# Four 32-column tiles for P·V and a second TensorE round for the sums, with PSUM laid out anew

## The chip, the core and the metric

The kernel runs on one core of a Trainium2 chip. The time is the device time of one execution in microseconds (us), as the median of three runs. TensorE (PE) multiplies matrices, VectorE (DVE) reduces and works elementwise, ScalarE (ACT) computes the exponentials, GpSimd (POOL) splits numbers into two parts, SyncE (SP) issues most DMAs.

## The reference

A decoder block in float32 on 4 batches of 1024 tokens, width 512, 16 heads of width 32. Three layers follow one another; each ends with a residual sum and a layer norm. The change touches the first two, which are attentions of one shape:

```python
# layer 0: gated self-attention
attn_align = softmax(einsum('bhqd,bhkd->bhqk', inner, outer) / sqrt(32))
attn = attn_align * aperture[b,h,q,None] * expression[b,h,None,k]   # both sigmoids of x @ W
attn = attn / (attn.sum(axis=-1, keepdims=True) + 1e-8)
converged = einsum('bhqk,bhkd->bhqd', attn, v)                      # then turned and multiplied by Wout
# layer 1: cross-attention on ctx, keys masked
scores = where(mask == 0, -inf-like, q @ k.T / sqrt(32)); p = softmax(scores); out = (p @ v) @ Wo
# layer 2: experts, gates and one causal attention; untouched
```

## The kernel before

`attention(nc, masked, io)` is written once and built twice: layer 0 (`masked` false) and layer 1. Each has a loop over the 4 batches, and in it every engine walks the same list, `attention_steps(masked)`, and does its part of each step. So the order of the list is the order on every engine, and semaphores join the engines.

In a batch come the projections (`Q`, `K`, `V`, and in layer 0 `EX`, `AP` for the gates), each 512-wide product held in one PSUM bank; then 8 pairs of heads; then the output projection `out`, and the transposes `xt` for the next layer.

A pair `p` has 8 steps over the keys, `kt`, of 128 keys each. In one such step stand:
- `st`, two heads: the transposed scores, 128 keys by 1024 queries, 2 matmuls of 512 columns a head (L557); in layer 1 each is followed by a matmul that adds the mask (L562). ACT takes the exponential of 1024 columns at once into `probs` (L781). A ring of two 1024-wide tiles, `scores`, holds them.
- `smax`: the scores the other way round for the next pair, to find each query's maximum. 2 heads by 8 blocks by 2 halves make 32 single matmuls a pair (L627), each into one bank of the 512-wide ring `work`, and DVE reduces each (L977; in layer 1 L973 with the mask). In pair 0 they run at 1 or 2 a gap, since they must be ready ahead; in pairs 6 and 7 they run out.
- `pv`: `v_ext` (32 columns of V, and 2 that give sums) times `probs`, for one half `c` of the queries and both heads, in two tiles of 64 columns (L580). Between the halves stands an `smax`.

After a pair, DVE copies the accumulators to `u` (L859). `den` turns them by 4 transposes a half, so that the sums lie along the partitions (L637); DVE makes 1/sum (L1007 to L1025); `bc` turns that back, spread over 32 rows (L644); DVE multiplies (L1033) into `q_raw`. The last pair's `den` and `bc` run with nothing beside them, and POOL's split (L403, L405) and the `out` step wait for them. In layer 1 DVE adds a correction for absent rows (L995) in pair 7.

`mneg` (L631) turns the maxima into one row, which ACT copies and a DMA puts into the stack for the next pair's `st`.

The matmuls of the projections, `st` and `smax` have float32r operands; `pv`, `den`, `bc` and `mneg` have float32, and the profile records a 512-wide float32 product as two matmuls (2048 in the code, 4096 in the profile).

Of the kernel before, what the change touches and what calls it, by code (L numbers as in the profile page):

```python
# [15 lines left out]
VW = DH + 2  # L16
# [18 lines left out]
def attention_steps(masked):  # L35

    smax = lambda p: [("smax", p, h, t, c) for h in range(2) for t in range(TT) for c in range(NC_)]  # L40
# [18 lines left out]

    GAPS = 4  # L60
    ahead = [m for p in range(1, PAIRS) for m in smax(p)]
    left = 0
    due = []
    for p in range(PAIRS):
        extra = {}
        if p > 0:
# [1728 lines left out]
```

## Time and profile before

| what | value |
|---|---|
| median of 3 runs (lowest, highest) | 5076.81 us (5066.39, 5081.88) |
| profiled execution, first to last instruction | 5068.7 us |
| PE busy | 4480.0 us, 88% |
| DVE busy | 2950.8 us, 58% |
| ACT busy | 1400.0 us, 28% |
| POOL busy | 734.8 us, 14% |
| mean granted TensorE clock | 0.944 of full |

Layers 0 and 1 take the span up to about 4000 us, layer 2 the rest. A matmul's recorded duration holds its latency, and matmuls overlap, so the distance from one start to the next says what one costs, and the busy share overstates how full PE is. An engine's idle time counts only where PE, the engine that is nearly always busy, waits for it.

### The profile page before, as it was taken

What the parts mean: (1) busy time and instruction counts of PE and PEld (TensorE: products, weight loads), DVE (VectorE), ACT (ScalarE), POOL (GpSimd) and SP (SyncE); (2) the same over time, 40 slices, a digit from 0 to 9 for tenths busy, and PEclk for the clock granted to TensorE, in tenths of its full rate; (3) what the DMA queues carried; (4) which work ended last, traced back from release to release, by engine and by line L of the source; (5) the groups of instructions that cost most, each with busy time, mean ns of one, the idle gap of its engine ahead of it and who ended that gap; (6) DMA issues with size and microseconds to landing.
All of it is one profiled execution on the core that took longest, in us unless ns stands there. A gap on an engine that the chain in (4) does not pass through costs nothing. (4 is left out here: it accounts for less than half of the span.)

```text
span 5068.7 us, 60158 instructions
## 1 busy us (share of the span) xinstructions
PE 4480.0 (88%) x19080; PEld 2464.3 (49%) x19080; DVE 2950.8 (58%) x5751; ACT 1400.0 (28%) x1693; POOL 734.8 (14%) x488
## 2 busy tenths in 40 slices
PE   6898899789988977999799979997999598989897
PEld 4334533543363335333543354335433276767676
DVE  3674476367546743664466546653665475757575
ACT  1333234223413421333133312341233302020202
POOL 2102210320021013102210131003100100000000
PEclk9999999899999988999899989998999798999998
DMA  2212211221122214210421042114211300000000
GB/s 81 59 39 73 65 38 51 69 57 38 38 80 59 55 45 139 51 38 26 162 59 37 27 154 57 37 38 144 65 38 30 125 11 33 18 33 19 34 17 17
DMA packets 114496, 285.92 MB, mean 56 GB/s; under 512 B 16240, under 2 KB 18160, under 8 KB 114160
## 3 DMA queue, kind: packets, MB, share of 16 engines
q1 hardware_dynamic: 87648, 213.54, 16.1%
q10 hardware_dynamic: 26512, 68.16, 3.9%
q8 instruction: 178, 2.92, 0.2%
q14 instruction: 158, 1.29, 0.1%
HBM read 137.48 MB, written 42.99 MB: 36 GB/s over the span
## 5 line engine op out<-in xcount | busy, mean ns | idle before, releaser
L781 ACT ACTIVATE probs<-scores 128x1024 f32<-128x1024 f32 x1024 | 1027.3, 1023 | 1637.0 <-PE scores L562 880.0
L580 PE MATMUL acc<-probs,v_ext 128*34 128x512 f32 x4096 | 1064.0, 606 | 1.0 <-DVE u L859 1.0
L627 PE MATMUL work<-stack 96*128 96x512 f32 x1792 | 876.8, 497 | 91.4 <-DVE q_raw L1033 31.2
L973 DVE CUSTOM_DVE_ANT_0 work<-work,mask_q 128x512 f32<-128x512 f32 x896 | 619.8, 704 | 327.9 <-PE work L627 305.2
L557 PE MATMUL scores<-stack 97*128 97x512 f32 x2048 | 785.3, 458 | 4.0 <-ACT probs L781 2.6
L977 DVE TENSOR_REDUCE mx<-work 128x1 f32<-128x512 f32 x896 | 602.8, 689 | 267.1 <-PE work L627 256.0
L627 PEld LDWEIGHTS work<-stack 96*128 96x128 f32 x1792 | 336.9, 190 | 820.3 <-issue 381.2
L518 PE MATMUL work<-stack,w 128*128 128x512 f32 x1536 | 382.7, 411 | 172.8 <-DVEq L871 152.1
L1336 PE MATMUL work_e<-w_in_e,x_e 128*128 128x512 f32 x2304 | 523.4, 389 | 0.0
L1336 PEld LDWEIGHTS work_e<-w_in_e,x_e 128*128 128x128 f32 x2304 | 432.2, 188 | 89.8
L557 PEld LDWEIGHTS scores<-stack 97*128 97x128 f32 x2048 | 396.0, 195 | 102.1 <-ACT probs L781 51.2
L518 PEld LDWEIGHTS work<-stack,w 128*128 128x128 f32 x1536 | 302.6, 199 | 251.0 <-DVEq L871 155.2
L562 PE MATMUL scores<-mask_k,eye 128*128 128x512 fp8e5 x1024 | 406.9, 397 | 0.0
L403 POOL TENSOR_SCALAR qk<-q_raw 128x512 fp32r<-128x512 f32 (+1 forms) x96 | 73.5, 766 | 2120.2 <-DVEq L1038 980.8
L580 PEld LDWEIGHTS acc<-probs,v_ext 128*34 128x34 f32 x4096 | 159.8, 110 | 321.7 <-issue 278.5
L518 PE MATMUL work<-w,qk 128*128 128x512 f32 x768 | 207.8, 423 | 42.8 <-POOL qk L405 27.6
L562 PEld LDWEIGHTS scores<-mask_k,eye 128*128 128x128 fp8e5 x1024 | 101.1, 99 | 274.8 <-issue 274.2
L1336 PE MATMUL work_e<-w_out_e,mixed_t_e 128*128 128x512 f32 x768 | 204.2, 426 | 17.1 <-DVEq L1685 17.1
L1033 DVE TENSOR_TENSOR q_raw<-u,work 32x512 f32<-32x512 f32 x256 | 173.9, 679 | 73.2 <-PE work L644 68.8
L518 PE MATMUL work<-w,stack 128*128 128x512 f32 x768 | 203.8, 419 | 7.6 <-POOLq L438 4.7
L859 DVE COPY u<-acc 128x512 f32<-128x512 f32 x128 | 82.5, 686 | 211.2 <-PE acc L580 211.2
L518 PEld LDWEIGHTS work<-w,qk 128*128 128x128 f32 x768 | 150.4, 203 | 99.2 <-issue 67.9
(228 smaller groups left out, 3974.6 us busy)
## 6 DMA issues: line engine op xcount, KB each, us to landing
stack<-qk SPq DMA_DIRECT2D x384, 256.0 KB, 4.9
stage<-x_t SPq DMA_DIRECT2D x32, 512.0 KB, 3.5
k_raw<-x SPq DMA_DIRECT2D x8, 2048.0 KB, 8.6
x_t<-xts ACTq DMA_DIRECT2D x16, 1024.0 KB, 6.8
x<-k_raw ACTq DMA_DIRECT2D x8, 2048.0 KB, 8.2
mstage<-mask ACTq DMA_DIRECT2D x32, 512.0 KB, 3.8
mstage<-mask_t ACTq DMA_DIRECT2D x32, 512.0 KB, 3.5
kv_raw<-ctx_t SPq DMA_DIRECT2D x4, 2048.0 KB, 7.9
```

Source lines behind the costliest of these rows:

```text
L403: pool.tensor_scalar(hi, raw, 1.0, 0.0, ALU.mult, ALU.add)
L518: last = pe.matmul(out, a(k), b(k), start=(k == 0 and n == 0), stop=(k == KT - 1 and n == 2))
L557: last = pe.matmul(scores[n % 2][:, c * CH:(c + 1) * CH], stack[0:3 * DH + 1, s, 2 + h, kt * P:(kt + 1) * P], stack[0:3 * DH + 1, s, h, c ...
L562: last = pe.matmul(scores[n % 2][:, c * CH:(c + 1) * CH], eye8[:, :], mask_k[:, kt, c * CH:(c + 1) * CH], start=False, stop=True)
L580: last = pe.matmul(acc[64 * h:64 * h + VW, c, :], v_ext[:, kt, 2 * p + h, :], probs[:, n % PRING, c * CH:(c + 1) * CH], start=(kt == 0), s ...
L627: last = pe.matmul(bank[:, :], stack[0:3 * DH, s, h, t * P:(t + 1) * P], stack[0:3 * DH, s, 2 + h, c * CH:(c + 1) * CH], start=True, stop= ...
L781: act.activation(probs[:, n % PRING, :], scores[n % 2][:, :], ACT.Exp, scale=SCALE).then_inc(p_full, 1)
L859: dve.tensor_copy(u[:, c, :], acc[:, c, :]).then_inc(u_ready, 1)
L973: dve.tensor_tensor_reduce(bank[:, :], bank[:, :], mask_q[:, t, c * CH:(c + 1) * CH], 1.0, -3e38, ALU.add, ALU.max, mx[:, p % 2, j:j + 1]) ...
L977: dve.tensor_reduce(mx[:, p % 2, j:j + 1], bank[:, :], AX.X, ALU.max).then_inc(free, 1)
L1033: last = dve.tensor_tensor(q_raw[a:a + DH, p // 2, c * CH:(c + 1) * CH], u[64 * h:64 * h + DH, c, :], bank[DH * h:DH * (h + 1), :], ALU.mult)
L1336: last = pe.matmul(out, a(k), b(k), start=(k == 0 and n == 0), stop=(k == tiles - 1 and n == 2))
```

## The change

- `pv` is one step for all four products of a `kt` (2 heads, 2 halves), each in a tile of 32 columns of its own, into one bank of `acc`. The columns of sums leave `v`; a second round of four matmuls, with `ones` (layer 1) or `e_one` (layer 0: expression and one) as weights, puts the sums into the other bank, at the same partitions.
- `den` and `bc` are gone. In layer 1 the sums stand on all 32 rows of a tile, and DVE takes maximum, reciprocal and product at 512 columns. In layer 0 a matmul with a selection matrix (`sel`) spreads the two sums over 32 rows; 1/aperture goes out to DRAM and comes back spread by 4 DMAs a pair.
- PSUM: `scores` becomes `wides`, for `sm` (an `smax` of 1024 columns), `mneg`, `sel`, `RZ`; `work` becomes `halfs`, for the projections and for `st`, whose exponentials are now 512 wide.
- In a `kt` the order is: `st` of head 0, two `sm` (three in pair 0), `st` of head 1, `mneg` or `sel` if due, `pv` of the `kt` before.
- The correction of absent rows moves from pair 7 into each `out` step.

```diff
@@ attention_steps
+    smax = lambda p: [("sm", p, h, t) for h in range(2) for t in range(TT)]
         for kt in range(TT):
             before = (p, kt - 1) if kt else (p - 1, TT - 1)
+            steps += [("st", p, kt, 0, c) for c in range(NC_)]
+            misc = due
+            due = []
+            rate = (0 if kt == 0 else 3) if p == 0 else 2
+            for _ in range(rate):
+                if ahead:
+                    m = ahead.pop(0)
+                    steps.append(m)
+                    if m[2:] == (1, TT - 1):
+                        due.append(("mneg", m[1]))
+            steps += [("st", p, kt, 1, c) for c in range(NC_)]
+            steps += misc
+            if masked and p == 2 and kt == 4:
+                steps.append(("RZ",))
+            if not masked and p > 0 and kt == 2:
+                steps.append(("sel", p - 1))
+            if before[0] >= 0:
+                steps.append(("pv", *before))
@@ tensor
+                    if kind == "pv":
+                        _, p, kt = step
                         for c in range(NC_):
+                            half_emptied(pe, i, ("st", p, kt, 1, c))
+                        if kt == 0:
+                            pe.wait_ge(u_ready, 1 + i * PAIRS + p)
+                        for c in range(NC_):
+                            for h in range(2):
+                                j = 2 * c + h
+                                last = pe.matmul(acc[DH * j:DH * (j + 1), 0, :], v[:, kt, 2 * p + h, :],
+                                                 probs[:, kt % 2 * 2 + h, c * CH:(c + 1) * CH],
+                                                 start=(kt == 0), stop=(kt == TT - 1), skip_group_check=True)
+                        if masked:
...
+                                    last = pe.matmul(acc[DH * j:DH * (j + 1), 1, :], ones[:, :],
...
+                        else:
...
+                                    last = pe.matmul(acc[DH * j:DH * j + 2, 1, :], e_one[:, kt, 2 * p + h, :],
...
+                        elif kind == "sel":
+                            pe.wait_ge(u_ready, 1 + i * PAIRS + step[1] + 1)
+                            for part in range(2):
+                                last = pe.matmul(bank[:, part * CH:(part + 1) * CH], sel[:, part, :], u[:, 1, :],
+                                                 start=True, stop=True)
-                        for t in range(HALF):
-                            last = pe.transpose(bank[:, t * P:(t + 1) * P], u[:, c, t * P:(t + 1) * P], eye[:, :])
@@ scalar
-                        act.activation(probs[:, n % PRING, :], scores[n % 2][:, :], ACT.Exp,
-                                       scale=SCALE).then_inc(p_full, 1)
+                        act.activation(probs[:, kt % 2 * 2 + h, c * CH:(c + 1) * CH], bank[:, :], ACT.Exp,
+                                       scale=SCALE).then_inc(free, 1)
@@ vector
+                def normalise(p, over):
+
+                    a = 2 * DH * (p % 2)
                     for c in range(NC_):
+                        rows = slice(2 * DH * c, 2 * DH * (c + 1))
+                        last = dve.tensor_tensor(q_raw[a:a + 2 * DH, p // 2, c * CH:(c + 1) * CH], u[rows, 0, :],
+                                                 over[rows, :], ALU.mult)
+                    elif kind == "pv":
+                        if step[2] == TT - 1:
+                            p = step[1]
+                            take_acc(p)
+                            if masked:
+                                dve.tensor_scalar(u[:, 1, :], acc[:, 1, :], 1e-30, None, ALU.max)\
+                                   .then_inc(sums_taken, 1)
+                                dve.drain()
+                                dve.reciprocal(u[:, 1, :], u[:, 1, :])
+                                dve.drain()
+                                normalise(p, u[:, 1, :])
+                    elif kind == "sel":
...
+                        dve.scalar_tensor_tensor(out=den[:, :], in0=bank[:, CH:S], scalar=1e-8, in1=over_a[:, p % 2, :],
+                                                 op0=ALU.mult, op1=ALU.mult).then_inc(over_used, 1)
+                        dve.drain()
+                        dve.tensor_tensor(den[:, :], bank[:, 0:CH], den[:, :], ALU.add).then_inc(free, 1)
+                        dve.drain()
+                        dve.reciprocal(den[:, :], den[:, :])
+                        dve.drain()
+                        normalise(p, den[:, :])
+                    elif kind == "out":
...
                         if masked:
+                            dve.scalar_tensor_tensor(out=y[:, t, :], in0=rz[:, :], scalar=none[:, t:t + 1],
+                                                     in1=y[:, t, :], op0=ALU.mult, op1=ALU.add)
                             dve.drain()
```

What PE issues in one `kt` in the middle of a pair of layer 0, before: two `st` heads (L557), the two halves of `pv` (L580), and a single `smax` (L627) in each gap.

```order
L557 MATMUL scores_0<-stack_49 128x512 [waits p_full_0]
L557 MATMUL scores_0<-stack_49 128x512
L588 REGISTER_ALU
L627 MATMUL work_0<-stack_49 128x512 [waits work_free0_0]
L555 REGISTER_ALU
L557 MATMUL scores_0<-stack_49 128x512 [waits p_full_0]
L557 MATMUL scores_0<-stack_49 128x512
L627 MATMUL work_0<-stack_49 128x512 [waits work_free1_0]
L580 MATMUL acc<-probs_55,v_ext_53 34x512 [waits p_full_0]
L580 MATMUL acc<-probs_55,v_ext_53 34x512
```

The same `kt` in the changed kernel, up to its `pv` (L568, then the sums L585, which stand here from the `kt` before).

```order
L568 MATMUL acc<-probs_55,v_53 32x512 x3
L585 MATMUL acc<-probs_55,e_one_76 2x512 x4
L634 MATMUL half_0<-stack_49 128x512 [waits half_free1_0]
L623 REGISTER_ALU
L634 MATMUL half_0<-stack_49 128x512 [waits half_free0_0]
L593 REGISTER_ALU
L600 MATMUL wide_0<-stack_49 128x512 [waits wide_free0_0]
L600 MATMUL wide_0<-stack_49 128x512
L600 MATMUL wide_0<-stack_49 128x512 [waits wide_free1_0]
L600 MATMUL wide_0<-stack_49 128x512
L634 MATMUL half_0<-stack_49 128x512 [waits half_free1_0]
L623 REGISTER_ALU
```

The two `pv` groups, which `smax` parted, now stand together as one run of eight; every `st` matmul waits for its own bank (`half_free`), and the maxima come in pairs of two banks.

What DVE does from the end of a pair of layer 0, before: the copy of `acc` (L859), maxima (L977) and the short operations of `den` (L1016 to L1025) on 8 or 256 columns.

```order
L859 COPY u_58<-acc 128x512 [waits pv_done_0]
L859 COPY u_58<-acc 128x512
L977 TENSOR_REDUCE mx_63<-work_0 128x1 [waits work_full1_0]
L269 REGISTER_ALU
L977 TENSOR_REDUCE mx_63<-work_0 128x1 [waits work_full0_0]
L977 TENSOR_REDUCE mx_63<-work_0 128x1 [waits work_full1_0]
L269 REGISTER_ALU
L1016 TENSOR_TENSOR r_59<-work_0,gate_75 128x8 [waits work_full0_0]
L1018 SCALAR_TENSOR_TENSOR r_59<-work_0,r_59 128x8
L1021 RECIPROCAL r_59<-r_59 128x8
L1023 TENSOR_TENSOR r_59<-r_59,gate_75 128x8
L1025 COPY r_wide_60<-r_59 128x256
```

The same place after: two maxima (L1006) for each of two `kt`, then `sel` (L1035) and its chain at 512 columns, with the next `kt`'s maxima behind it.

```order
L894 COPY u_58<-acc 128x1024 [waits pv_done_0]
L1006 TENSOR_REDUCE mx_61<-wide_0 128x1 [waits wide_full1_0]
L267 REGISTER_ALU
L1006 TENSOR_REDUCE mx_61<-wide_0 128x1 [waits wide_full0_0]
L1006 TENSOR_REDUCE mx_61<-wide_0 128x1 [waits wide_full1_0]
L267 REGISTER_ALU
L1006 TENSOR_REDUCE mx_61<-wide_0 128x1 [waits wide_full0_0]
L1035 SCALAR_TENSOR_TENSOR den_79<-wide_0,over_a_77 128x512 [waits wide_full1_0,over_in1_0]
L1038 TENSOR_TENSOR den_79<-wide_0,den_79 128x512
L1040 RECIPROCAL den_79<-den_79 128x512
L901 TENSOR_TENSOR q_raw_50<-u_58,den_79 64x512 x2
L267 REGISTER_ALU
```

The reciprocal moved from 8 columns to 512, and it now stands in one block between maxima.

## Rows read from the trace of the kernel before

**Rows 1.** The page: the span, and each engine's busy time.
```profile
span 5068.7 us, 60158 instructions
PE 4480.0 (88%) x19080; PEld 2464.3 (49%) x19080; DVE 2950.8 (58%) x5751; ACT 1400.0 (28%) x1693; POOL 734.8 (14%) x488
```

**Rows 2.** Busy time by window, columns in the first line: pair 5, a stage, pair 7, a stage.
```profile
core 0: us, PE busy (x) PEld busy (x) DVE busy (x) ACT busy (x) POOL busy (x), PEclk, DMA share, GB/s
349.90:389.10 39.20, 37.52 (x147) 15.16 (x148) 27.69 (x50) 15.98 (x17) 0.00 (x0) 1.00 0.21 65
597.00:909.20 312.20, 288.82 (x1118) 115.44 (x1118) 197.72 (x344) 128.88 (x136) 30.96 (x18) 0.98 0.21 50
2351.00:2381.90 30.90, 30.89 (x136) 10.86 (x136) 11.00 (x22) 14.96 (x15) 0.00 (x0) 1.00 0.00 1
2553.60:2903.80 350.20, 345.38 (x1385) 127.87 (x1386) 218.38 (x571) 133.15 (x137) 37.66 (x24) 0.99 0.17 39
```

**Rows 3.** Timeline of PE (start, length, count in one row): `V`, then pair 7.
```profile
131.54 3.04 PE L518 MATMUL work<-w,stack 128*128 128x512 f32 x12 [0.46 <-DVE v_ext L928]
...
440.59 1.19 PE L557 MATMUL scores<-stack 97*128 97x512 f32 x4
441.71 1.91 PE L580 MATMUL acc<-probs,v_ext 128*34 128x512 f32 x8
443.55 1.19 PE L557 MATMUL scores<-stack 97*128 97x512 f32 x4
```

**Rows 4.** Timeline of PE: two `pv` groups of another pair, parted by `smax`.
```profile
709.91 1.05 PE L580 MATMUL acc<-probs,v_ext 128*34 128x512 f32 x4
710.89 0.50 PE L627 MATMUL work<-stack 96*128 96x512 f32 x1
711.33 1.05 PE L580 MATMUL acc<-probs,v_ext 128*34 128x512 f32 x4
```

**Rows 5.** Timeline of PE in layer 2: four float32 matmuls in one 32-column tile.
```profile
4032.44 1.88 PE L1350 MATMUL work_e<-squares_e,ones_e 128*32 128x512 f32 x4 [0.32 <-issue]
```

**Rows 6.** Groups of DVE's instructions by form: count, busy us, mean ns.
```profile
L859 DVE COPY u<-acc 128x512 f32<-128x512 f32 x128 | 82.5, 686 | 211.2 <-PE acc L580 211.2
L959 DVE CUSTOM_DVE_ANT_0 scores<-scores,mask_q 128x1024 f32<-128x1024 f32 x64 | 77.1, 1248 | 1.5 <-PE scores L536 1.5
L963 DVE TENSOR_REDUCE mx<-scores 128x1 f32<-128x1024 f32 x64 | 75.2, 1216 | 27.1 <-PE scores L536 27.1
L944 DVE RECIPROCAL gate_t<-gate_t 32x512 f32<-32x512 f32 x8 | 26.7, 3341 | 0.6
L995 DVE SCALAR_TENSOR_TENSOR k_raw<-rz,none,k_raw 128x512 f32<-128x512 f32 x32 | 21.6, 745 | 0.1
```

**Rows 7.** Groups of ACT's instructions by form.
```profile
L781 ACT ACTIVATE probs<-scores 128x1024 f32<-128x1024 f32 x1024 | 1027.3, 1023 | 1637.0 <-PE scores L562 880.0 <-PE scores L557 746.7 <-issue 0.9
L796 ACT ACTIVATE xts<-work 128x512 f32<-128x512 f32 x64 | 36.9, 594 | 23.6 <-PE work L670 23.1
```

**Rows 8.** Timeline at the end of pair 7: layer 0, then (from 2381) layer 1.
```profile
446.85 1.46 PE L580 MATMUL acc<-probs,v_ext 128*34 128x512 f32 x6
...
448.36 1.29 DVE L859 COPY u<-acc 128x512 f32<-128x512 f32 x2 [14.06 <-PE acc L580]
...
454.33 0.62 POOL L403 TENSOR_SCALAR qk<-q_raw 128x512 fp32r<-128x512 f32 x1 [175.16 <-DVEq L1038]
...
2381.94 1.29 DVE L859 COPY u<-acc 128x512 f32<-128x512 f32 x2 [12.39 <-PE acc L580]
...
2387.42 0.62 POOL L403 TENSOR_SCALAR qk<-q_raw 128x512 fp32r<-128x512 f32 x1 [70.02 <-DVEq L1038]
```

**Rows 9.** Timeline of pair 0, then the waits of PE from 150 to 447 us.
```profile
144.50 0.76 PE L627 MATMUL work<-stack 96*128 96x512 f32 x1 [7.00 <-DMA stack<-qk]
...
PE work L627 <- DVE mx L977: 5.5, 13, 1.0
PE work L627 <- DVE q_raw L1033: 4.6, 6, 0.8
```

**Rows 10.** Timeline: DVE's 8-column product beside POOL's work, and without it.
```profile
272.97 2.37 POOL L405 TENSOR_TENSOR qk<-q_raw,qk 128x1024 fp32r<-128x1024 f32 x1
273.62 1.75 DVE L1023 TENSOR_TENSOR r<-r,gate 128x8 f32<-128x8 f32 x1
...
450.57 0.17 DVE L1023 TENSOR_TENSOR r<-r,gate 128x8 f32<-128x8 f32 x1
```

More of the change, by code:

```diff
@@ L46, in attention_steps @@
     rest += [("V", t) for t in range(TT)]
-    first = [("smax0", h, t) for h in range(2) for t in range(TT)]
+    first = smax(0)
     lead = 6
@@ L98, in attention_steps @@
     steps += [("xt", t) for t in range(TT)]
-    if sum(s[0] not in ("st", "pv", "smax0") for s in steps) % 2:
-        steps.append(("pad",))
-    return steps
+    for kinds, name in ((WIDE_KINDS, "wpad"), (HALF_KINDS, "xpad")):
+        if sum(s[0] in kinds for s in steps) % 2:
+            steps.append((name,))
+    return steps
+WIDE_KINDS = ("sm", "mneg", "sel", "RZ", "wpad")
+HALF_KINDS = ("Q", "K", "EX", "AP", "V", "CS", "st", "out", "xt", "xpad")
 def attention(nc, masked, io):
     steps = attention_steps(masked)
-    uses = [s for s in steps if s[0] not in ("st", "pv", "smax0")]
@@ L193, in attention @@
         psum = lambda n, shape: ctx.enter_context(nc.psum_tensor(f"{n}_{int(masked)}", shape, F32))
-        work = [psum(f"work{b}", [P, CH]) for b in range(2)]
-        scores = [psum(f"scores{b}", [P, S]) for b in range(2)]
-        acc = psum("acc", [P, NC_, CH])
+        wides = [psum(f"wide{b}", [P, S]) for b in range(2)]
+        halfs = [psum(f"half{b}", [P, CH]) for b in range(2)]
+        acc = psum("acc", [P, 2, CH])
         const_in = sem("const_in")
@@ L244, in attention @@
             bo_added = sem("bo_added")
+            sums_taken = sem("sums_taken")
         else:
@@ L586, in _ @@
-                    n = use_no[step]
-                    bank = work[n % 2]
-                    pe.wait_ge(work_free[n % 2], 1 + i * PER + n // 2)
-                    if kind in ("Q", "K"):
+                        last = pe.matmul(bank[:, :],
+                                         stack[0:3 * DH + 1, s, 2 + h, kt * P:(kt + 1) * P],
+                                         stack[0:3 * DH + 1, s, h, c * CH:(c + 1) * CH],
+                                         start=True, stop=not masked)
@@ L590, in _ @@
+                        if masked:
+                            last = pe.matmul(bank[:, :], eye8[:, :], mask_k[:, kt, c * CH:(c + 1) * CH],
+                                             start=False, stop=True)
+                    elif kind in ("Q", "K"):
                         _, g, c = step
```

438 lines of the change are left out of this document (189 added, 249 removed).

## The prediction

> **What bounds the kernel now.** I read the page first: PE is busy 88% of the span, no other engine over 58% [rows 1]. The windows then say where: from the first `st` to the last `pv` of a batch ("a stage") layer 0 takes 312.2 us and layer 1 350.2, with PE busy in 289 and 345 of them at clocks of 0.98 and 0.99 [rows 2]. Eight stages are 2650 us, over half the span, and the change lives in them and in what follows each. So PE's own issue time bounds the stages, and I need the price of a matmul from starts, not durations.
>
> **Unit prices** (all us). Twelve float32r matmuls of 512 columns take 3.04, of which the last one's latency is about 0.40: (3.04-0.40)/11 = 0.24; I use 0.235 [rows 3]. Eight `pv` records take 1.91 and a `kt` of pair 7 takes 443.55-440.59 = 2.96 [rows 3]. Four float32 records in one tile take 1.88 [rows 5], four in two tiles 1.05 [rows 4]: two tiles run beside each other, and one round (two records at once) costs 1.88-1.05 = 0.83 over two rounds, so 0.42 to 0.43. Of the 2.96, four `st` are 0.94 and four rounds 1.71; the other 0.31 is what entering and leaving the narrow tiles costs. With one `smax` between two groups the distance is 711.33-709.91 = 1.42 = 0.235 + 0.855 + 0.33 [rows 4]: the same. I take 0.32 for each run of `pv`. The Trainium skill ("TensorEngine Tiling (Array Packing)", Key Properties) says a change of tiling mode drains the engine; by that, one switch fewer is one drain fewer, and the trace agrees with its 0.3.
>
> In layer 1, pair 7 takes 30.9 [rows 2]; less 8 x (1.71+0.32) = 16.2, 64 `st` and mask matmuls are 0.23 each.
>
> **Check on the kernel before**, a stage of layer 0: 256 `st` x 0.235 = 60.2; 224 `smax` x 0.235 = 52.6; 128 groups x (0.855+0.32) = 150.4 less 3 for those that join; transposes and `mneg` some 22 (my estimate); the wait of 7.0 for the stack's DMA [rows 9]; half speed, 2% of 312, 5. Sum 294; the other 18 are waits for DVE, of which one batch's rows show 10 ahead of `smax` [rows 9].
>
> **PE work of the stage after.** Per `kt` one run of 16 records. If four tiles run at once, that is 4 x 0.427 + 0.32 = 2.03, where before two runs cost 2.35. The price of four at once is in no row. From below: four cost what two do (0.427 a round), since two start within one row and finish in 1.05. From above: they run in pairs, 3.42 + 0.32 a `kt`; or one by one (1.88 for four), 6.8. I take the low end, being nearest to what tiles do here [rows 4].
> - Layer 0: 60.2 + 52.6 + 64 x 2.03 = 129.9; `sel`, 4 float32 records of 0.43, x 7 = 12.0; `mneg` 2.5. Sum 257.
> - Layer 1: 512 x 0.23 = 117.8; 52.6; 129.9; `mneg` 2.5; `RZ` 12 x 0.235 = 2.8. Sum 305.6.
>
> **Waits of PE after.** Results reach DVE or ACT some 0.5 after a matmul's start, and a freed bank reaches PE within 0.1.
> - *Three `sm` in a `kt` of pair 0, two banks.* The first `sm` starts 0.47 (layer 1: 0.93) into the `kt` and DVE ends it 1.22 (1.25) later [rows 6]: at 2.46 (2.96). PE wants the bank at 1.41 (1.88). Wait 1.15 (1.2), seven times: 8.0 (8.4).
> - *The chain after a pair, layer 1.* `acc` is complete 4.84 into the pair's first `kt` after it: copy 0.69, maximum 0.6, reciprocal 3.34, two products 1.4 (priced as `u`'s copy) [rows 6]. DVE is free at 10.95. The maxima of `kt` 1 lie in both banks; at `kt` 2 PE wants one at 10.6 and gets it at 12.3, then the next at 13.45 instead of 12.77. Wait 2.4, six pairs: 14.4. Before, this was short operations on 8 columns.
> - *Layer 0.* The copy (1.22) is over before `pv` of `kt` 1. `sel` at `kt` 2 needs the bank of an `sm` just issued: 0.7. Then 0.75 + 0.7 + 3.34 + 1.4 [rows 6] from 12.5 to 18.7, and at `kt` 4 PE waits 1.3 and 0.67. Together 2.67, six pairs: 16.
> - *No `sm` between the `st`* (`kt` 0, and 10 `kt` of pairs 6 and 7). The second head needs the bank whose exponential has just begun: 0.59 for 512 columns (a copy's price) against 1.02 for 1024 [rows 7]. PE wants it at 0.57 and 1.41, gets it at 1.15 and 1.68: 0.88 x 11 = 9.7. In layer 1 the mask matmuls cover half: 0.5 x 11 = 5.5. Before, pair 7 had no such wait [rows 3].
> - *As before:* 7.0 for the DMA in pair 0 of layer 0, and low clock, 5 (layer 0) and 1.5.
>
> The stages come to 257 + 8 + 16 + 9.7 + 12 = 302.5 and 305.6 + 28.3 + 1.5 = 335.4; they fall by 9.7 and 14.8. ACT has 4 x 0.59 = 2.4 a `kt` of at least 3.9, DVE 2 x 1.22 a `kt` and some 8 a pair of 36: both fit, save for the block above.
>
> **After the stage.** Before, POOL's first split starts 454.33-448.36 = 5.97 after `u`'s copy in layer 0 and 5.48 in layer 1 [rows 8]. After, layer 0: copy 1.22, `sel` 2.1 with latency, 0.75, 0.7, 3.34, product 0.7, handovers 0.2 = 9.0: +3.0 a batch. Layer 1: 0.6 + 0.7 + 3.34 + 0.7 + 0.1 = 5.4: even.
>
> **`out` of layer 1.** The 8 corrections (L995), 0.745 each [rows 6], were hidden in pair 7. Now each stands ahead of the sum in `out`, four of them where DVE holds the end of the batch: 3 us. DVE's operation on two SBUF operands waited for POOL's, 1.75 instead of 0.17, until POOL's row ended (273.62+1.75 = 272.97+2.37 roughly) [rows 10]; POOL splits beside `out`, so I add 1: +4 a batch, bounds 0 (hidden) and 8 x (0.75+1.26) = 16 (all exposed, each behind a POOL operation of 1.26).
>
> The Trainium skill ("SBUF — State Buffer", SBUF: two separate sides) has an exclusive lock between GpSimd and a VectorE operation with two SBUF inputs. The rows agree; by that rule every correction beside a split would wait, and the sum would be up to 12 a batch higher.
>
> The DMAs that spread 1/aperture (4 a pair, 64 KB each) cost nothing: they are issued a pair ahead, on SP, behind the stack's; were they late, `sel`'s chain would wait and with it the maxima. Projections and layer 2 keep their work: 0.
>
> **Sum.** 4 x (-9.7 - 14.8 + 3.0 + 4) = -70. On the profiled 5068.7 that is 4999; this execution lies 8 below the median of the runs, 5076.8, so 5007.
>
> **Rivals.**
> 1. *Four tiles run two at a time.* For it: no row has four tiles at work, only two. Against: nothing in two tiles' 1.05 hints at a shared limit. Price 2 x 0.855 x 512 `kt` = +875: 5881. It decides early: 70/(512 x 4) = 0.034 us more a round of four already eats the gain.
> 2. *Four tiles overlap only in part*, a round at 0.56. 4 x 0.13 x 512 = +270: 5276. The Trainium skill ("TensorE: Matmul & The Clock Gate", Part 3) measured 3.07 times for four row tiles, not four times, and 2.38 for three column tiles; taken as a sustained rate that is 0.427 x 4/3.07 = 0.556. Taken as one isolated pack with its latency, it says nothing against the forecast; the two-tile rows here lose only 0.02 a group, so I think the latter.
> 3. *DVE's long block takes PE's place.* Place: `kt` 1 to 4 of each pair, reciprocal and products. If each of the 48 pairs loses 3 us more than I have (POOL holding DVE as in rows 10, and the clock falling in the wait), +144: 5150, slower. It decides from 70/48 = 1.5 us a pair. Against: a stage's clock is 0.98 though PE waits for DVE now [rows 2, 9].
> 4. *No change:* waits of 1.5 us a pair more, and the gain is gone: 5077.
> 5. *More gain:* PE gets ahead in the `kt` after a wait, half of the 62 us of waits a batch vanish: -124, 4882.
>
> **How the numbers follow.** Forecast 0.52 (4950 to 5060), rival 1 0.08, rival 2 0.06, rival 3 0.12, rival 4 0.12, rival 5 0.10. A measurement of this kernel tells 0.3%, 15 us, from no change. Faster: 0.52 + 0.10 = 0.62. Same 0.13, slower 0.25. The range leaves out rivals 1 and 2 and a little at the low end: 4900 to 5150; that of the likeliest case alone is 4950 to 5060.
>
> **What would show it.** Right: records of `acc` starting four at a time, 0.43 apart, 16 in about 1.9; stages near 302 and 335; PE waits for DVE's maxima at `kt` 2 and 4; POOL's first split 9 after the copy in layer 0. Wrong: a round of four over 0.5 (rivals 1, 2); waits over 4 a pair on DVE, or a clock under 0.95 in a stage (rival 3); DVE's reciprocal of 128 rows far from the 3.34 of 32 rows.

## The result, and the profile after

The changed kernel takes 5141.65 us (median of 4 runs, 5128.05 to 5149.32), the kernel before 5071.6 beside it: a ratio of 1.0132, 95% interval 1.0108 to 1.0157. It is slower by 1.3%, clear of noise, where a gain of 70 us, to 5007, was forecast. The profiled execution went from 5068.7 [rows 1] to

```profile
span 5134.1 us, 63734 instructions
...
PE 4363.3 (85%) x22296; PEld 2486.5 (48%) x22296; DVE 2812.4 (55%) x3736; ACT 1493.4 (29%) x2717; POOL 747.7 (15%) x488
```

PE is busy 117 us less and the span is 65 longer. So PE was given less to do, and waiting took more than its place. The windows say where: a stage of layer 0 and one of layer 1 (the same two as in [rows 2], where the columns are named), then a piece of the second, from within `kt` 2 of pair 1.

```profile
601.50:916.40 314.90, 283.09 (x1546) 116.41 (x1546) 182.74 (x155) 142.06 (x264) 30.84 (x18) 0.96 0.23 56
2579.70:2939.60 359.90, 327.11 (x1785) 135.86 (x1786) 190.64 (x269) 143.16 (x265) 39.36 (x24) 0.96 0.17 39
2648.60:2654.00 5.40, 5.40 (x19) 1.94 (x22) 2.63 (x6) 1.19 (x2) 0.00 (x0) 0.52 0.00 0
```

Layer 0 stands at 312 to 315 (312.2 before), layer 1 at 359.9 (350.2 before), and the mean clock of both stages fell to 0.96. In layer 1 PE is idle 33 of the 360. What it waits for there (total, times, longest):

```profile
PE wide L600 <- DVE mx L1002: 27.6, 17, 4.7
PE half L634 <- ACT probs L811: 2.9, 10, 0.3
```

DVE's maxima are 28 of it. The time from one `st` of head 0 to the same of the next `kt` shows that these waits stand in pair 0 and in one single `kt` of each of pairs 1 to 6 (stage from 2579.7; in us, `kt` 0 to 7; "low" is the time of TensorE at half clock in that pair; pair 7 has no `sm` and no such `kt`):

```
pair 0  3.87 7.55  6.67 6.66 6.66 6.67 6.67 7.72   low 5.8
pair 1  4.81 4.83 12.76 4.84 4.83 4.83 5.31 4.83   low 6.8
pair 2  4.83 4.83  7.68 4.84 8.07 4.84 5.35 4.83   low 0
pair 3  4.83 4.83 12.69 4.83 4.83 4.83 5.31 4.83   low 6.8
pair 4  4.83 4.83  7.68 4.84 4.83 4.83 5.31 4.84   low 0
pair 5  4.83 4.83  9.20 4.85 4.83 4.83 5.31 4.84   low 3.4
pair 6  4.83 4.83 12.41 4.86 4.83 4.50 4.68 4.50   low 6.8
```

The plain `kt` is 4.83, what the forecast's unit prices give (4.81). The 8.07 of pair 2 holds `RZ`, and each 5.3 holds `mneg`. `kt` 2 is the place. Here it is in pair 2, where POOL is idle: DVE's copy of `u`, maximum, reciprocal, products, the next maximum, and PE's `sm` that waits for it (timeline; start, length).

```profile
2684.28 0.69 DVE L892 COPY u<-acc 128x512 f32<-128x512 f32 x1 [0.75 <-PE acc L577]
...
2684.89 0.68 DVE L1023 TENSOR_SCALAR u<-acc 128x512 f32<-128x512 f32 x1
2685.66 3.35 DVE L1026 RECIPROCAL u<-u 128x512 f32<-128x512 f32 x1
...
2689.09 1.39 DVE L901 TENSOR_TENSOR q_raw<-u 64x512 f32<-64x512 f32 x2
...
2690.49 1.23 DVE L1002 CUSTOM_DVE_ANT_0 wide<-wide,mask_q 128x1024 f32<-128x1024 f32 x1
...
2691.88 0.73 PE L600 MATMUL wide<-stack 96*128 96x512 f32 x2 [1.83 <-DVE mx L1002]
```

And in pair 1, where POOL splits group 2 of `q_raw` and `k_raw` at the same time:

```profile
2638.61 3.35 DVE L1026 RECIPROCAL u<-u 128x512 f32<-128x512 f32 x1
...
2641.93 2.36 POOL L438 TENSOR_TENSOR qk<-q_raw,qk 128x1024 fp32r<-128x1024 f32 x1
2642.03 4.24 DVE L901 TENSOR_TENSOR q_raw<-u 64x512 f32<-64x512 f32 x2
...
2644.44 1.29 POOL L436 TENSOR_SCALAR qk<-k_raw 128x1024 fp32r<-128x1024 f32 x1 [0.16 <-issue]
...
2645.88 2.60 POOL L438 TENSOR_TENSOR qk<-k_raw,qk 128x1024 fp32r<-128x1024 f32 x1
2646.28 1.23 DVE L1002 CUSTOM_DVE_ANT_0 wide<-wide,mask_q 128x1024 f32<-128x1024 f32 x1
...
2647.63 2.40 PE L600 MATMUL wide<-stack 96*128 96x512 f32 x4 [4.63 <-DVE mx L1002]
```

The two products take 4.24 instead of 1.39. Taken one by one, the first takes 2.79 and ends at 2644.82, 0.53 behind POOL's two-operand operation (2644.29); the second takes 1.43 and ends at 2646.27, 0.54 behind POOL's next one (2645.73), which reads one operand. Alone one takes 0.69, so each runs nearly whole behind the end of POOL's operation. PE waits 4.63 instead of 1.83. The clock falls to half at 2646.95, still in this wait, and stays there for 6.8: the window 2648.6 to 2654.0 above has a granted clock of 0.52, and the four matmuls of two `sm` take 2.40, where at full clock they take 1.28. POOL's splits for groups 2 and 3 always begin at the start of pairs 1 and 3 (they wait for the stack's DMAs, which wait for the pair before), and its eight additions of `bo` (11.7 from 2860.7) fall into pair 6, where the products take 3.08: three collisions a stage of layer 1.

The parts that answer to the other rows of before: a run of `pv` of all four tiles [rows 3, 4],

```profile
2687.01 1.07 PE L568 MATMUL acc<-probs,v 128*32 128x512 f32 x8
2687.89 1.04 PE L577 MATMUL acc<-probs,ones 128*32 128x512 f32 x8
```

(0.88 from the start of the first round to the sums, 0.97 on to the next `st`; 1.85 in all, forecast 2.03. By the same measure two `pv` groups took 2 x 1.19: 1.42 less the `smax`'s 0.235); DVE's new forms [rows 6],

```profile
L1026 DVE RECIPROCAL u<-u 128x512 f32<-128x512 f32 x32 | 107.3, 3353 | 2.9
...
L901 DVE TENSOR_TENSOR q_raw<-u 64x512 f32<-64x512 f32 x64 | 72.6, 1134 | 3.2
...
L1053 DVE SCALAR_TENSOR_TENSOR k_raw<-rz,none,k_raw 128x512 f32<-128x512 f32 x32 | 29.0, 905 | 39.8 <-PE half L549 39.8
```

and the tail of layer 0, then of layer 1 [rows 8].

```profile
449.28 1.23 DVE L894 COPY u<-acc 128x1024 f32<-128x1024 f32 x1 [17.27 <-PE acc L585]
...
450.56 1.98 PE L610 MATMUL wide<-u,sel 128*128 128x512 f32 x4 [1.46 <-DVE u L894]
...
454.28 3.35 DVE L1040 RECIPROCAL den<-den 128x512 f32<-128x512 f32 x1
457.71 1.49 DVE L901 TENSOR_TENSOR q_raw<-u,den 64x512 f32<-64x512 f32 x2
458.61 1.07 POOL L436 TENSOR_SCALAR qk<-q_raw 128x512 fp32r<-128x512 f32 x1 [182.93 <-DVEq L904]
```

```profile
2404.85 0.69 DVE L892 COPY u<-acc 128x512 f32<-128x512 f32 x1 [27.08 <-PE acc L577]
...
2410.55 1.07 POOL L436 TENSOR_SCALAR qk<-q_raw 128x512 fp32r<-128x512 f32 x1 [73.37 <-DVEq L904]
```

From the copy to POOL's first split it is 9.33 and 5.70.

### The profile page after: what moved, and what is told of

The parts are those of the page before. It is cut to its first block and busy times, and to the rows that moved or that the text cites. A ratio compares the mean times of both kernels' runs of the same rounds, so it can differ in the third digit from the quotient of the medians.

```text
span 5134.1 us, 63734 instructions
## 1 busy us (share of the span) xinstructions
PE 4363.3 (85%) x22296; PEld 2486.5 (48%) x22296; DVE 2812.4 (55%) x3736; ACT 1493.4 (29%) x2717; POOL 747.7 (15%) x488
## 5 line engine op out<-in xcount | busy, mean ns | idle before, releaser
L811 ACT ACTIVATE probs<-half 128x512 f32<-128x512 f32 x2048 | 1115.4, 595 | 1584.2 <-PE half L639 892.7
L634 PE MATMUL half<-stack 97*128 97x512 f32 x2048 | 883.1, 493 | 43.0 <-ACT probs L811 33.1
L1002 DVE CUSTOM_DVE_ANT_0 wide<-wide,mask_q 128x1024 f32<-128x1024 f32 x512 | 618.5, 1247 | 484.5 <-PE wide L600 482.9
L600 PE MATMUL wide<-stack 96*128 96x512 f32 x2048 | 652.4, 434 | 238.0 <-DVE mx L1002 135.3
L1006 DVE TENSOR_REDUCE mx<-wide 128x1 f32<-128x1024 f32 x512 | 601.9, 1217 | 347.8 <-PE wide L600 344.3
L634 PEld LDWEIGHTS half<-stack 97*128 97x128 f32 x2048 | 380.3, 195 | 603.7 <-issue 442.4
L568 PE MATMUL acc<-probs,v 128*32 128x512 f32 x4096 | 571.4, 627 | 0.0
L600 PEld LDWEIGHTS wide<-stack 96*128 96x128 f32 x2048 | 384.8, 196 | 383.9 <-DVE mx L1002 176.9
L549 PE MATMUL half<-stack,w 128*128 128x512 f32 x1536 | 379.3, 408 | 177.3 <-DVEq L917 159.0
L639 PE MATMUL half<-mask_k,eye 128*128 128x512 fp8e5 x1024 | 413.9, 404 | 0.0
L585 PE MATMUL acc<-probs,e_one 128*2 128x512 f32 x2048 | 274.3, 604 | 0.0
L1348 PE MATMUL work_e<-w_out_e,mixed_t_e 128*128 128x512 f32 x768 | 207.6, 432 | 17.1 <-DVEq L1697 17.1
```

The source lines that it names most:

```text
L549: last = pe.matmul(out, a(k), b(k), start=(k == 0 and n == 0), stop=(k == KT - 1 and n == 2))
L568: last = pe.matmul(acc[DH * j:DH * (j + 1), 0, :], v[:, kt, 2 * p + h, :], probs[:, kt % 2 * 2 + h, c * CH:(c + 1) * CH], start=(kt == 0), ...
L585: last = pe.matmul(acc[DH * j:DH * j + 2, 1, :], e_one[:, kt, 2 * p + h, :], probs[:, kt % 2 * 2 + h, c * CH:(c + 1) * CH], start=(kt == 0 ...
L600: last = pe.matmul(bank[:, c * CH:(c + 1) * CH], stack[0:3 * DH, s, h, t * P:(t + 1) * P], stack[0:3 * DH, s, 2 + h, c * CH:(c + 1) * CH], ...
L634: last = pe.matmul(bank[:, :], stack[0:3 * DH + 1, s, 2 + h, kt * P:(kt + 1) * P], stack[0:3 * DH + 1, s, h, c * CH:(c + 1) * CH], start=T ...
L639: last = pe.matmul(bank[:, :], eye8[:, :], mask_k[:, kt, c * CH:(c + 1) * CH], start=False, stop=True)
```

## Experiments

All are compared with the kernel before, run beside them. "Stage" is first `st` to last `pv` in the profiled run, the mean of the four batches. `x_recip` and `p_double` give wrong results: the one leaves out the division by the sums, the other counts P·V twice.

| kernel | us | ratio to before, 95% | stage, layer 0 | layer 1 |
|---|---|---|---|---|
| before | 5071.6 | | 312.4 | 350.0 |
| after | 5141.65 | 1.0132 [1.0108, 1.0157] | 313.3 | 359.7 |
| x_apart | 5108.37 | 1.0063 [1.0047, 1.0080] | 311.4 | 353.8 |
| x_busy | 5152.82 | 1.0159 [1.0142, 1.0176] | 312.5 | 359.3 |
| x_recip | 4948.52 | 0.9756 [0.9740, 0.9772] | 298.8 | 329.1 |
| x_pieces | 4952.43 | 0.9766 [0.9750, 0.9782] | 298.4 | 326.3 |
| p_third | 4911.74 | 0.9678 [0.9662, 0.9694] | 293.9 | 319.9 |
| p_split | 4926.98 | 0.9713 [0.9697, 0.9730] | 292.9 | 323.6 |
| p_tail | 4919.91 | 0.9697 [0.9681, 0.9714] | 298.8 | 326.0 |
| x_all | 4845.59 | 0.9548 [0.9532, 0.9564] | 288.2 | 317.5 |
| x_late | 4876.73 | 0.9619 [0.9603, 0.9635] | 292.0 | 323.1 |
| p_double | 5396.33 | 1.0640 [1.0619, 1.0661] | 352.2 | 380.4 |

**x_apart: POOL's work held back.** A new semaphore counts the pairs whose products are done.

```diff
+                    if g >= 2:
+                        pool.wait_ge(products, i * PAIRS + 2 * g - 3)
...
+                    pool.wait_ge(products, i * PAIRS + 6)   # ahead of the additions of bo
```

> POOL's splits of q and k for groups 2 and 3 and its eight additions of bo are held back until DVE's products of pair 0, 2 and 5 have ended; nothing else moves. Theory A (the miss comes from DVE's products running beside POOL's long operations: 4.24 us instead of 1.39 in pairs 1, 3 and 6 of a layer 1 stage, then 6.8 us at half clock): kt 2 of pairs 1, 3 and 6 falls from 12.5 to about 8, the products there take 1.4, a layer 1 stage falls from 359.7 to 345, layer 0 by 1 to 3, the kernel by 50 to 70 against the kernel after (about 5142), to 5080. Rival B (the clock falls for the DVE wait alone, collision or not): kt 2 keeps its half clock, at most -20. Rival C (the reciprocal, not its neighbour, is the cost): no change within 10.

```profile
2628.44 1.38 DVE L907 TENSOR_TENSOR q_raw<-u 64x512 f32<-64x512 f32 x2
...
2630.03 1.05 POOL L437 TENSOR_SCALAR qk<-q_raw 128x1024 fp32r<-128x1024 f32 x1 [47.86 <-DVEq L911]
...
2631.43 0.78 PE L606 MATMUL wide<-stack 96*128 96x512 f32 x2 [2.03 <-DVE mx L1009]
```

The products are back at 1.38 in all pairs and POOL starts behind them. PE's wait falls to 2.03. But the time falls by 33 us only, and a stage of layer 1 by 5.9, not 15. Theory A named a true cost and made it too large by about two, for the low clock stays (24 to 32 us of a stage, mean clock 0.97):

```profile
2566.60:2919.70 353.10, 325.43 (x1787) 134.76 (x1787) 185.79 (x269) 143.15 (x265) 37.77 (x24) 0.97 0.17 39
```

In this stage pairs 3 and 6 have a `kt` 2 of 7.9 at full clock, while pairs 1, 2, 4 and 5 have 9.5 to 10.8 with 3.4 or 6.8 at half clock. So rival B is partly right: an idle wait of 2 us can be followed by half clock without any collision. (Pair 5 in the table above shows it too.) The edit is not quite neutral: it adds a `drain` of DVE behind the products, the maxima start 0.34 behind them instead of 0.01, and `kt` 2 at full clock is 7.93 where it was 7.68, 1.5 more in a stage. In the stage of the table above, `kt` 2 thus splits into its parts: 4.83; +2.85 for the wait behind the block; for a collision what the products take longer, +2.9 in pairs 1 and 3 and +1.7 in pair 6, 7.4 in all; the rest, +1.5 for a stretch of 3.4 and +2.1 to 3.0 for one of 6.8, is half clock. 7.4 less 1.5 is the 5.9 measured here.

**x_busy: PE kept at work in the wait.**

```diff
+                        for _ in range(12 if masked and p in (1, 3, 6) and (kt, h, c) == (2, 0, 1) else 0):
+                            pe.matmul(bank[:, :], stack[0:3 * DH + 1, s, 2, kt * P:(kt + 1) * P],
+                                      stack[0:3 * DH + 1, s, 0, c * CH:(c + 1) * CH], start=True, stop=True)
```

> In layer 1, kt 2 of pairs 1, 3 and 6, twelve more matmuls (a repeat of the st matmul of head 0, columns 512 to 1023, overwritten by the real one) stand where PE waits for DVE, 2.8 us of work in a wait of 4.6. Theory A (half of what a hit pair costs is PE at half clock after the idle wait): no low clock after kt 2 of these pairs, kt 2 stays at 12.5 less 3.4, each hit pair -3.4 or so, the kernel -30 to -45 against after. Rival (the low clock costs nothing since PE waits anyway, or comes whatever PE does): within 10, or up to +20 when the extra matmuls push the exponentials back.

The first stage of layer 1 goes the way of theory A: the low clock falls from 32 us to 12 (`kt` 2 of pairs 3 and 6 at 9.9 and 9.3 instead of 11.5 and 12.2, none of it at half clock), and the stage from 359.4 to 353.3. (The fill takes up most of a wait and not all: 2.0, 1.3 and 0.8 of it are left in pairs 1, 3 and 6. At full clock `kt` 2 is longer by 2.3 and 1.7 in pairs 3 and 6 than the 7.61 of pair 5, and the products there are longer by 2.3 and 1.7.) In the next stage pairs 2, 4 and 5, whose wait was left as it was, ran at half clock for 6.8 each, and so did pair 3, filled as it was:

```profile
2037.10:2390.40 353.30, 328.31 (x1823) 139.97 (x1822) 190.58 (x269) 143.28 (x265) 39.31 (x24) 0.98 0.17 39
2566.00:2930.40 364.40, 340.46 (x1823) 143.58 (x1822) 190.68 (x269) 143.71 (x265) 39.49 (x24) 0.95 0.16 38
```

Over the whole kernel nothing was gained (1.0159 against 1.0132, and the intervals overlap), where theory A had 30 to 45. The low clock costs time where it comes: `kt` 2 of pair 2 is 7.67 in the first stage and 9.30 with 3.4 at half clock in the last, behind the same wait of 1.83. But which of the equal waits it follows wasn't steered by filling some of them. What decides that stays open.

**x_recip: the long operation left out.** `dve.reciprocal` of 128x512 is replaced in both layers by one multiply-and-add of 0.7 us.

> Both layers' reciprocal of 128x512 is left out (replaced by one elementwise operation that gives a constant), so the output isn't normalised; its length falls from 3.34 to about 0.7, all else stands. Theory A (the DVE chain of copy, maximum, reciprocal, products at the start of a pair is what PE waits for at kt 2 to 4): the waits for the maxima outside pair 0 go, a layer 1 stage -20, layer 0 -10, and 2.6 less behind each stage: the kernel -120 to -160 against after, to about 5000. Rival (collisions with POOL alone): the products still collide, the clock still falls, -40 to -70. Rival (the base time of a kt and pair 0): -20 at most beside the tail's 21.

```profile
584.30:883.20 298.90, 276.54 (x1546) 116.23 (x1546) 165.06 (x155) 141.99 (x264) 30.90 (x18) 0.98 0.25 59
2479.70:2807.40 327.70, 313.59 (x1788) 132.95 (x1786) 167.63 (x269) 142.76 (x265) 38.55 (x24) 0.99 0.18 42
```

-193 us against after, more than theory A's 120 to 160, and the last rival is out. `kt` 2 is 4.83 in pairs 1 to 5 and 6.7 in pair 6; the clock is back at 0.98 and 0.99. The collisions of pairs 1 and 3 are gone as well, since the products now come before POOL's splits (1.37 for the two); only pair 6 keeps its own (3.28). So this run takes out the block's length and two of three collisions together. That collisions alone aren't the cost is shown by pairs 2, 4 and 5, which have none and lose their waits here, and by x_apart.

**x_pieces: the same work in four pieces.** Reciprocal and products of a pair are cut into 128 columns each, one piece behind the maxima of `kt` 2 to 5 (layer 1) or 3 to 6 (layer 0).

```diff
+            if p > 0 and kt in at:
+                steps.append(("nm", p - 1, at.index(kt)))
...
+                def piece(p, j):
+                    dve.reciprocal(over[:, cols], over[:, cols])
...
+                        dve.tensor_tensor(q_raw[a:a + 2 * DH, p // 2, c * CH + j * P:c * CH + (j + 1) * P],
+                                          u[rows, 0, cols], over[rows, cols], ALU.mult)
```

> The reciprocal and the two products of pairs 0 to 6 are cut in four pieces of 128 columns, one behind the maxima of kt 2, 3, 4, 5 (layer 1) and 3, 4, 5, 6 (layer 0); the last pair is as it was. Theory A (the length of DVE's block in one piece makes PE wait): a piece of 1.4 to 1.6 fits beside the 2.5 of maxima of a kt of 4.0 and 4.8, the waits at kt 2 go, no half clock outside pair 0, a layer 1 stage -20 (to 340), layer 0 -8 (to 304 to 306): the kernel -90 to -110 against after, to 5030 to 5050. Rival (cutting costs more in start-up than it saves: each piece over 2.2): DVE falls behind in every kt, no gain or up to +50.

```profile
586.30:885.20 298.90, 276.19 (x1542) 116.44 (x1546) 192.31 (x218) 142.02 (x264) 30.89 (x18) 0.98 0.25 59
2487.00:2813.30 326.30, 313.43 (x1788) 133.52 (x1788) 191.95 (x332) 142.77 (x265) 37.88 (x24) 0.99 0.18 43
```

All of the work is done and it is as fast as without the reciprocal: -189 us, where theory A had 90 to 110, and 2.3% faster than before. A stage of layer 1 falls by 33 and not by 20, since collisions and half clock go with the wait. The edit changes two things, the length of the block and its place behind the maxima of the `kt`; no run moves the block whole. A piece of this stage, one that even runs beside POOL:

```profile
2552.98 2.37 POOL L441 TENSOR_TENSOR qk<-k_raw,qk 128x1024 fp32r<-128x1024 f32 x1
...
2553.25 0.95 DVE L904 RECIPROCAL u<-u 128x128 f32<-128x128 f32 x1
...
2554.27 1.52 DVE L909 TENSOR_TENSOR q_raw<-u 64x128 f32<-64x128 f32 x2
...
2554.73 1.28 PE L605 MATMUL wide<-stack 96*128 96x512 f32 x4
```

The collision costs this piece 1 us (1.52 for two products of 128 columns, 0.59 elsewhere), and PE's `sm` at 2554.73 doesn't wait, since DVE has 2.3 us a `kt` to spare. What is left of PE's waits for DVE is pair 0's (and 1.3 ahead of `mneg`):

```profile
PE wide L605 <- DVE mx L1021: 7.5, 7, 1.1
```

**p_third: the third `sm` of pair 0.** On top of x_pieces, it goes behind the `st` of head 1.

```diff
+            for n in range(max(rate, 2)):
+                if n == 2:
+                    steps += [("st", p, kt, 1, c) for c in range(NC_)]
```

> On top of the kernel with the reciprocal in pieces (4952): the third sm of a kt of pair 0 stands behind st of head 1 instead of in front of it. Theory A (the third sm wants the bank of the first, whose maximum ends 1.2 later than PE asks; 7 times a stage): a kt of pair 0 falls from 6.67 to about 5.3 (4.83 and one sm of 0.47) in layer 1 and from 5.5 to 4.6 in layer 0, a stage -9 and -5 to -6, the kernel -50 to -60, to about 4895. Rival (DVE's own pace, 3 maxima of 1.25 and their gaps, bounds a kt of pair 0): 3.8 to 4 is below 5.3, so only if the exponentials or the next kt's first sm then wait: gain under 20.

-41 us, where theory A had 50 to 60. A `kt` of pair 0 falls from 6.67 to 5.72, not to 5.3 (layer 0: 5.51 to 5.03, not to 4.6), and the wait for DVE (7.5 and 1.3 above) to

```profile
PE wide L613 <- DVE mx L1024: 1.8, 6, 0.5
PE wide L608 <- DVE mx L1024: 0.9, 6, 0.2
```

Theory A's wait is the cause; a third of it is left.

**p_split: the rounds on either side of `st`.** On top of x_pieces, where no `sm` stands between the two heads.

```diff
+                if steps[-1][0] == "st" and before[0] >= 0:
+                    steps.append(("pa", *before))      # P.V; the sums stay behind
```

> On top of the kernel with the reciprocal in pieces (4952): in the 11 kt of a stage that have no sm between the two heads' st (kt 0 of pair 0 has no P.V either) the round of P.V stands between them and the round of sums behind, at the price of entering the narrow tiles a second time (0.32). Theory A (PE waits there for ACT's exponential of the bank just filled): a kt of pair 7 falls from 4.03 to about 3.3 in layer 0 and from 4.51 to 4.2 in layer 1, a stage -7 to -8 and -3, the kernel -40 to -45. Rival (ACT's four exponentials and handovers bound these kt at 4.0 and 4.5): no change within 10. Rival (each change of tiles costs much more than 0.32 here): up to +20.

-25 us, where theory A had 40 to 45. A plain `kt` of pair 7 falls from 4.03 to 3.29 and from 4.50 to 4.25, as theory A has it. The stage of layer 0 gains 5.5 instead of 7 to 8, because `kt` 1 of pair 7 takes 4.60, longer than the 4.03 of x_pieces: the P.V round, now a `st` earlier, waits for DVE's copy of the pair before (this row is from x_all, which has the same edit).

```profile
PE acc L577 <- DVE u L907: 1.2, 1, 1.2
```

The stages gain 32 in all. From one stage of layer 1 to the next it is 178.8 here and 175.4 in x_pieces, which takes the difference back; no run says why.

**p_tail: the last pair in pieces too, the corrections of `y` back in pair 7.** On top of x_pieces.

```diff
-                    if t % (TT // NC_) == 0:
-                        pool.wait_ge(ctx_done, i * NC_ + t // (TT // NC_) + 1)
+                    if t < 4:
+                        pool.wait_ge(ctx_done, i * 4 + t + 1)
```

> On top of the kernel with the reciprocal in pieces (4952): the last pair's reciprocal and products are also done in four pieces, each of which lets POOL split one of the first four row tiles, and the eight corrections of y (layer 1) stand in the middle of pair 7 again. Theory A (each stage's tail runs through the whole reciprocal, and the corrections stand on DVE's path in the output stage): POOL's first split comes 7.2 behind the last round instead of 10.07 in layer 0 and 3.6 instead of 6.44 in layer 1, -2.8 x 8 = -22, and -3 x 4 for the corrections: the kernel -25 to -40. Rival (the output stage is bound by POOL's eight splits or by DVE later on, and what comes earlier waits there): under 10.

```profile
2304.13 0.69 DVE L896 COPY u<-acc 128x512 f32<-128x512 f32 x1 [20.07 <-PE acc L581]
...
2305.51 0.95 DVE L903 RECIPROCAL u<-u 128x128 f32<-128x128 f32 x1
2306.54 0.59 DVE L908 TENSOR_TENSOR q_raw<-u 64x128 f32<-64x128 f32 x2
...
2307.34 0.62 POOL L439 TENSOR_SCALAR qk<-q_raw 128x512 fp32r<-128x512 f32 x1 [64.01 <-DVEq L911]
...
2308.27 1.55 DVE L908 TENSOR_TENSOR q_raw<-u 64x128 f32<-64x128 f32 x2
```

-33 us, inside theory A's range, but partly by luck: of the profiled 32, 11.5 fall in layer 2, whose code is the same (1064.4 in x_pieces, 1052.9 here, with 163 and 142 us of it at half clock). Outside layer 2 it is 20, less than the 25 to 40. POOL starts 3.21 behind the copy instead of 5.70 (the second piece's products, 1.55, run into POOL's split again).

**x_all: the four edits together.**

> The four edits together: reciprocal in pieces in all pairs, third sm moved, round of P.V between the st where no sm stands, corrections in pair 7. Each acts on other kt or on the tail, so theory A says they add: 4952 less 55, 43 and 32 = about 4820. Rival (what one edit gives PE is taken back by the next bound, ACT in layer 0's kt or the clock): 4870 or more.

```profile
574.40:862.60 288.20, 273.39 (x1543) 114.08 (x1546) 192.31 (x218) 142.02 (x264) 30.90 (x18) 0.98 0.25 61
2428.00:2745.20 317.20, 313.38 (x1784) 130.94 (x1787) 200.31 (x340) 142.87 (x265) 37.91 (x24) 0.99 0.19 44
```

4845.6: 107 less than x_pieces, where the three single edits add up to 99. By the stages they add, as theory A says: 76 us where p_third and p_split alone gave 44 and 32. Outside the stages the profiled sums move by up to 12 us from run to run in layer 2 alone, so the agreement of 107 and 99 says no more. 4820 was too low by what p_split and p_third had already given less than forecast. It is 4.5% faster than the kernel before and 5.8% than the changed one.

**x_late: the maxima of pair 1 a `kt` later.** On top of x_all; the table of `sm` per `kt` of pair 0 is 0, 0, 4, 3, 3, 3, 3, 3 in place of 0, 3, 3, and so on.

> On top of the four edits together (4846): in pair 0 the sm of pair 1 start one kt later (none in kt 1, four in kt 2, three a kt after it). Theory A (PE stands 6.2 in kt 1 of layer 0 for the stack's DMA with the exponentials and P.V of the kt behind it, and then works at half clock): kt 1 of layer 0 falls from 13.6 to 3.5, kt 2 rises from 5.05 to 11 or 12, 2 to 3 a stage in layer 0; in layer 1, where the DMA is early, the fourth sm of kt 2 waits for DVE, +1 to 2, and pair 0's lead in sm is 2 shorter, which moves two sm from pair 0 to pair 6: 0. The kernel -3 to -10. Rival (the DMA itself is tied to the work ahead of it and lands later too): 0 to +10.

+31 us, so the expectation failed, and its rival of 0 to +10 too. Pair 0 of layer 0 did fall, from 47.7 to between 44.2 and 45.1. But each of pairs 2 to 7, in both layers, begins with a wait that wasn't there:

```profile
PE half L647 <- DMA stack<-mrow: 4.9, 6, 1.7
```

The maxima of a pair, its `mneg` and the DMA of the row of maxima end two `sm` later, and `st` of the next pair waits for that DMA. I had priced the shorter lead at 0.

**p_double: the price of a round.** On top of x_pieces, the P.V round is issued twice in each `kt`.

> On top of the kernel with the reciprocal in pieces (4952): the P.V round of every kt is issued twice, so P.V is counted double; the sums are not. This prices one round of four tiles (eight float32 matmul records at full clock, 512 of them). Forecast of the prediction (four tiles cost what two cost, 0.427 a round of four, so 0.855 for the eight records): +0.87 to 0.9 a kt, 4952 + 512 x 0.88 = 5400 at most, less where the kt waited for ACT (11 kt of a stage, 1.06 in layer 0 and 0.3 in layer 1), so 5350 to 5400. Rival (tiles overlap in part, 0.56): +1.12 a kt, 5500 or more.

```profile
2779.48 1.92 PE L574 MATMUL acc<-probs,v 128*32 128x512 f32 x16
2781.22 1.04 PE L584 MATMUL acc<-probs,ones 128*32 128x512 f32 x8
```

Four rounds of four tiles take 1.74: 0.435 each, forecast 0.427. +444 us over 512 `kt` is 0.87 a `kt`, and 5396 lies in the forecast of 5350 to 5400. Rivals 1 and 2 of the prediction are out. The Trainium skill ("TensorE: Matmul & The Clock Gate", Part 3) gives 3.07 times for four row tiles; carried over to column tiles as a sustained rate, as rival 2 did, it does not hold here, where four cost per round what two cost.

## Why the prediction was wrong

- **Rival 3's mechanism came true**: DVE's long block takes PE's place. Both parts that it named are there, POOL holding DVE and the clock falling in the wait. It had a chance of 0.12 and a time of 5150; 5142 was measured, and this closeness is luck. It counted 3 us in each of 48 pairs, 144 in all. Measured are 3.2 in each of the 24 pairs of layer 1, 76, and 0.5 in those of layer 0; the rest came from elsewhere (below). One of its signs, a stage's clock under 0.95, did not show (0.96). The stated range up to 5150 holds the time, but the forecast itself was a gain, and the kernel lost.
- **The failed step** is "The chain after a pair, layer 1", 14.4 a stage. The wait itself is about right in size: 2.85 a pair, forecast 2.4. Its followers were left out, though a low clock stood among the stage's terms with 1.5. In the stage from 2579.7, `kt` 2 of the six pairs is 33.4 over its base: 17.1 for the waits, 7.4 for three collisions, and the other 8.9 for half clock. x_pieces takes out 33.4 by its stages (359.7 - 326.3). That is 19 a stage over the forecast, 76 in all. The miss is 135 (-70 forecast, +65 measured in the profiled time); the points on layer 0's chain and on the rest of the stages have the rest.
- **I had the evidence and used it elsewhere.** The lock between POOL and DVE was priced at `out` [rows 10], and not where the change puts 64-row products of two SBUF operands beside POOL's splits. The Trainium skill ("SBUF — State Buffer", SBUF: two separate sides) states that lock for every VectorE operation with two SBUF inputs beside a GpSimd one; the trace agrees, with 4.24 against 1.39, and also where POOL's operation reads one operand (1.43 against 0.69), which [rows 10] don't show. The kernel before had no such pair of inputs in this place: its products read `u` and PSUM. And I argued from a clock of 0.98 in waits of before, which averaged 0.4 and 0.8 and were 1.0 at most [rows 9]; the new waits for the first `sm` of `kt` 2 are 1.8 to 4.7. The length of one wait, and not their sum, was what differed.
- **Layer 0's chain** was near: 16 forecast, 4.2 of it for `sel`'s bank at `kt` 2 and 11.8 at `kt` 4. The pieces take out only the part at `kt` 4: 14.9 (313.3 - 298.4), of which 3 is half clock behind 6 of its 24 waits of 1.0 to 1.3. `kt` 2 stays, 2.26 over a plain one, where the forecast had 2.42. There are no collisions: the products come when POOL's splits are over, and the mean of one is 0.69, where it is 1.13 in layer 1 (72.6 for 64, above).
- **The rest of the stages was too cheap**, by 7.7 in layer 0 and 5.3 in layer 1 (298.4 against 302.5 less 11.8, and 326.3 against 335.4 less 14.4), 52 in all. In layer 0: 0.12 too little in 46 plain `kt` (4.03 against 3.91 by the unit prices) and 0.18 in the ten without `sm` (3.85), and the `kt` with `mneg` 0.7 longer six times where 2.5 in all stood. In layer 1 a `kt` of pair 0 waits 1.37 and not 1.2, one without `sm` takes 4.50 and not 4.37, and the clock is low for some 5.5 us of pair 0. With 76 and 52, and 12 for the 3.1 more at `kt` 4 of layer 0, this is 140 of a miss of 135; the last 5 went the other way, outside the stages, which grew by 22 and not by 28.
- **Right, by the runs:** four tiles at once (p_double); the wait for ACT in the `kt` without `sm` (brought down by p_split); the third `sm` as a wait (p_third); the tails, 9.33 and 5.70 against 9.0 and 5.4. From one stage to the next it is 2.8 longer in layer 0 and 3.2 in layer 1, forecast +3 and +4.

The idea of the change was sound. Its PE work is shorter (a plain `kt` takes 4.03 in layer 0 and 4.83 in layer 1, before 4.24 and 5.19), and with DVE's block in pieces it is worth -2.3%; as written, the single block of 6.2 us (copy, maximum, reciprocal, products) in DVE's queue ahead of the maxima costs more than it brings.

## What to carry to other kernels

When work moves onto an engine that another one waits for every few microseconds, ask for the longest uninterrupted block in its queue, not for its busy share: in layer 1, 6.2 us of DVE in one piece cost 33 us a stage; with the reciprocal and products in four pieces behind the maxima, `kt` 2 cost nothing extra. For each new operation on two SBUF operands, look up in the trace which POOL operation runs at that moment. And price a new wait of PE with what may follow it: here a stretch at half clock came behind some of the waits of 1.0 to 4.7 and cost 1.5 to 3.0 us more.

## What the runs showed that was not expected

- Two products of 64x512 took 1.38 alone and 4.24 beside POOL: 2.79 for the one beside a two-operand operation of 2.36, 1.43 for the one beside a one-operand operation of 1.29.
- In pairs 1 to 6 half clock came in stretches of 3.4 or 6.8 us behind waits, and not behind each: in the second stage of layer 1 of x_apart behind four of six of 2.0 to 2.2, in layer 0 of the changed kernel behind 6 of 24 of 1.0 to 1.3. With these waits gone (x_pieces), pairs 1 to 7 of that stage have none. Filling three of the waits (x_busy) took most of it away in one stage and not in the next.
- Layer 2, whose code is the same in all kernels, took 1053 to 1065 in the profiled runs, with 140 to 164 us of it at half clock. A difference of 10 us between two kernels need not come from the edit.
- The reciprocal costs 3.35 for 128x512 and 0.95 for 128x128, and the 32x512 of before 3.34 [rows 6]: it goes by columns, not by rows.
- A lead of the maxima shorter by two `sm` of 112 cost some 0.65 to 0.85 us at the start of pairs 2 to 7 in layer 1 (x_late: the `kt` ahead of it goes from 4.83 to between 5.95 and 6.16, of which 0.48 is `mneg`, which stood a `kt` earlier), by way of one small DMA.
